# Re-timed seams of a four-stage transformer layer: tree weights, widened reciprocals, normalization steps and diagonal masks

## The chip, the cores and the metric

One core of one Trainium2 chip runs one program. The metric is the device time in microseconds (us), the median of three runs. TensorE (PE) multiplies matrices into the eight banks of PSUM; VectorE (DVE), ScalarE (ACT) and GpSimd (POOL) do the rest; SyncE (SP), ACT and POOL issue DMAs. Each engine works through its own list in order, and semaphores tie the lists together.

## The reference, cut to what matters

```python
# x: 2 x 1024 x 256, context: 2 x 77 x 256, all fp32, 16 heads of 16
x = x + block(layernorm(x))         # causal self-attention (diagonal included), a scan of
                                    # 8 steps xs, vs <- tanh(ctx @ w_ctx + xs @ w_x + b), and an MLP
x = x + cross_attention(layernorm(x), context)
x = x + trees(layernorm(x))         # 8 binary trees of depth 7: silu(logit) * (node on path) @ W_out
# inside block:
scores = where(causal, -inf, q @ k.T / 4); attn = softmax(scores) @ v
x = x + (attn @ out_w + out_b); x = x + scan(layernorm(x))
x = x + gelu(layernorm(x) @ ff_w1 + ff_b1) @ ff_w2 + ff_b2
```

## The kernel before, in words

The program is one list of instructions per engine, written out by hand, over a transposed residual stream `res` of 2 x 128 partitions by 2048 tokens in four chunks (c = 0 to 3) of 512. Products that must be exact are done as three products of a high and a low part (`three`, lines 347 to 351), so weights and activations are split: one engine rounds to the high part and another subtracts to get the low part.

**Self-attention.** It runs in eight rounds (`XQUADS`, n = 0 to 7), each for four heads of one batch element. A round has 12 steps; a step computes scores on PE (L1743, twice two matmuls), exponentiates on ACT (L867), zeroes the upper triangle of diagonal blocks on POOL (L699) and weighs the values on PE (L1760). Beside this, the row maxima for the next rounds are found: `unit(n, u)` multiplies one 128 x 128 block of queries and keys for four heads into one of the banks 5, 6, 7 (L1721), and `maximum(n, u)` on DVE reduces the 128 x 512 bank to four columns of `part_max` (L1171). A round has 36 units, eight of them on the diagonal: u = 0, 2, 5, 9, 14, 20, 27, 35. For these, `unit` adds a second matmul (L1724) that accumulates the causal mask through an identity. The units of round n + 1 from u = 8 and the first eight (`LEAD`) of round n + 2 are spread over the steps of round n; `gather` (L1180) and `negate` (L1187) finish a round's maxima on DVE, with `turn`, a transpose on PE, between them. A unit waits until the bank's previous user, three before it, has been read.

**MLP.** For each chunk c, PE does eight units m of the first matmul (`ff1`, six matmuls each), ACT applies Gelu (L996) and rounds (`hid_hi`, L999), DVE subtracts (`hid_lo`, L1411), and PE does eight units k of the second matmul (`ff2`). The layernorm of a later chunk is run beside it: `total`, `mean`, `center` (L1114), `square` (L780), `total_squares` (L1123), `variance` (L1647), `deviation` (L788, a square root, for which ACT loads another table than for Gelu), `invert` (L1131), `spread_out` (L1662), `scale` (L1140), and for ln3 `third_high` and `third_low` (the split of the normalized rows). The place of each of them among m and k sets the order. In chunk 0 three layernorms (ln3 of chunks 1, 2 and 3) are in flight, and POOL adds `x0` (L729) and builds `kbd` and `xk2` (L734, L740).

**Cross-attention.** It has 16 steps g (two for each n). A step has scores, an exponential, `cross_unit` with `cross_max` (L1888, L1386) for round n + 2, and `cross_weigh` (L1920). SP loads the queries of n + 2 (`load_q`, L585, six DMAs), the negated maxima (`load_neg`, L591) and packs the numerators of n - 1 (`pack_values`, L611, four DMAs). For batch element 0 the softmax denominators come back without HBM: `invert_cross` takes reciprocals (L1458), `widen` multiplies them with `own_part` into 128 x 1024 (L1464, 1.23 us on DVE), `denominators(j)` on PE (L1933) adds them up by head with `same_head` as weights, and `normalize_part(j)` multiplies (L1483). `denominators(2)` and `(3)` need `widen(1)`. `cross_project` (L1946) follows from g = 11.

**Trees.** The weights of eight trees come by `load_tree(t)` (L598, 512 KB each) into buffers that earlier stages have left, and `split_weights(t)` on POOL splits them (L721, L723). `spread_cross(2)` and `(3)` are POOL's DMAs for batch element 1 (L750, L752).

## Time and profile before

| what | value |
|---|---|
| median of 3 runs | 894.53 us (893.73 to 896.83) |
| the profiled execution | 893.74 us, its span 892.0 us |
| PE busy | 865.2 us (97%) |
| DVE, ACT, POOL busy | 575.7, 489.6, 176.2 us |
| mean granted clock of TensorE | 0.998 of full speed |

The span is what the profile shows; 1.7 us of the profiled execution lie outside it. Each engine's busy time counts overlapping instructions once. A matmul's row lasts longer than its place in the queue: the distance to the next row's start is its slot.

### The profile page before, as it was taken

The numbers are of one execution on the slowest core, as the hardware profiler recorded it, in microseconds if no ns is written. First come the engines' busy times: TensorE is split into PE (matmuls) and PEld (weight loads), VectorE is DVE, ScalarE is ACT, GpSimd is POOL, SyncE is SP. The second block draws the span as 40 slices with busy tenths as digits, with TensorE's granted clock in tenths as the row PEclk, the third lists the DMA queues.
The fourth block names the chain that finished last, engine by engine and source line by source line (L and its number), as shares of the span: only waits on it lengthen the run. The fifth ranks groups of instructions, "written<-read, shape, count | busy, mean of one in ns | idle before, by whom it ended". The sixth has DMA issues, their size and how long they took to land.

```text
span 892.0 us, 11261 instructions
## 1 busy us (share of the span) xinstructions
PE 865.2 (97%) x3967; PEld 526.4 (59%) x3967; DVE 575.7 (65%) x864; ACT 489.6 (55%) x715; POOL 176.2 (20%) x207
## 2 busy tenths in 40 slices
PE   9999999999999999999999999999899999999998
PEld 4665545545455545544446778774345777777775
DVE  4778757757777426678878774366654566665554
ACT  3536566566566755766657555437657433444332
POOL 8712332323222311000011630000015700000000
PEclk9999999999999999999999999999999999999999
DMA  4314405515524114200000000114656200000000
GB/s 148 67 37 75 85 13 98 96 25 96 108 51 93 31 34 165 96 0 1 0 0 22 1 1 1 35 37 87 137 112 156 67 1 25 1 24 1 1 24 24
DMA packets 21879, 46.28 MB, mean 52 GB/s; under 512 B 7896, under 2 KB 10840, under 8 KB 21440
## 3 DMA queue, kind: packets, MB, share of 16 engines
q1 hardware_dynamic: 19136, 43.17, 21.4%
q10 hardware_dynamic: 2080, 1.27, 0.6%
q0 software_dynamic: 608, 1.12, 0.6%
q8 instruction: 33, 0.54, 0.3%
q14 instruction: 22, 0.18, 0.1%
HBM read 17.04 MB, written 2.29 MB: 22 GB/s over the span
## 4 chain that ended last, share of the span: by engine, by line
PE 84%; DVE 5%; ACT 3%; issue 2%; DMA 2%; POOL 1%; SPq 1%; ACTq 0%; DVEq 0%; POOLq 0%
PE psum L1959 12%; PE psum L1721 9%; PE psum L349 9%; PE psum L350 8%; PE psum L351 8%; PE psum L1760 8%; PE psum L1743 8%; PE psum L1687 3%; PE psum L1662 2%; PE psum L1873 2%; PE psum L1724 2%; PE psum L1647 1%; PE psum L1639 1%; PE psum L1946 1%; PE psum L2162 1%
## 5 line engine op out<-in xcount | busy, mean ns | idle before, releaser
L1171 DVE TENSOR_REDUCE part_max<-psum 128x4 f32<-128x512 f32 x288 | 185.5, 686 | 71.0 <-PE psum L1721 56.4
L867 ACT ACTIVATE prob<-psum 128x1024 f32<-128x1024 f32 (+1 forms) x192 | 145.4, 809 | 85.9 <-PE psum L1743 85.4
L1721 PE MATMUL psum<-k,nat_hi 128*128 128x512 f32 x288 | 119.0, 452 | 2.5 <-ACT nat_lo L814 1.2
L1743 PE MATMUL psum<-q,k 128*128 128x512 f32 (+3 forms) x384 | 96.3, 354 | 0.3 <-ACT prob L867 0.3
L1079 ACT ACTIVATE silu<-psum,wt_bias 128x512 f32<-128x512 f32 x64 | 40.5, 684 | 101.9 <-PE psum L351 93.7
L1721 PEld LDWEIGHTS psum<-k,nat_hi 128*128 128x128 f32 x288 | 50.9, 188 | 62.7 <-issue 50.7
L699 POOL TENSOR_SCALAR_AFFINE_SELECT prob<-prob 128x256 f32<-128x256 f32 x128 | 52.3, 415 | 166.0 <-ACT prob L867 164.8
L1760 PE MATMUL psum<-prob,vq 128*32 128x512 f32 (+3 forms) x768 | 81.8, 498 | 1.3 <-POOL prob L699 1.2
L1743 PEld LDWEIGHTS psum<-q,k 128*128 128x128 f32 x384 | 65.2, 189 | 20.5 <-ACT prob L867 8.6
L1580 DVE TENSOR_TENSOR masked_lo<-masked,masked_hi 128x1024 fp32r<-128x1024 f32 x32 | 41.4, 1295 | 42.1 <-ACT masked_hi L1086 42.1
L349 PE MATMUL psum<-masked_hi,wt_hi 128*128 128x512 f32 x128 | 56.2, 439 | 1.2 <-DVE masked_lo L1580 1.2
L1959 PE MATMUL psum<-nrm,early 128*128 128x512 f32 x128 | 57.1, 593 | 0.0
L1959 PE MATMUL psum<-act_u,early 128*128 128x512 f32 x128 | 57.1, 593 | 0.0
L349 PE MATMUL psum<-tree_hi,wt_hi 128*128 128x512 f32 x128 | 53.6, 419 | 3.5 <-POOL wt_lo L723 2.9
L350 PE MATMUL psum<-nrm_lo,wt_hi 128*128 128x512 f32 x128 | 50.3, 393 | 0.0
L351 PE MATMUL psum<-masked_hi,wt_lo 128*128 128x512 f32 x128 | 50.1, 391 | 0.0
L350 PE MATMUL psum<-masked_lo,wt_hi 128*128 128x512 f32 x128 | 49.9, 390 | 0.0
L351 PE MATMUL psum<-tree_hi,wt_lo 128*128 128x512 f32 x128 | 49.9, 390 | 0.0
L1569 DVE TENSOR_SCALAR decide<-psum,wt_bias 128x512 bf16<-128x512 f32 x32 | 24.0, 750 | 39.7 <-PE psum L351 39.6
L1959 PEld LDWEIGHTS psum<-nrm,early 128*128 128x128 f32 x128 | 24.2, 190 | 29.7 <-issue 29.7
L1959 PEld LDWEIGHTS psum<-act_u,early 128*128 128x128 f32 x128 | 24.2, 190 | 29.7 <-issue 29.7
L1386 DVE TENSOR_REDUCE xrow_max<-psum 128x4 f32<-128x312 f32 x64 | 29.0, 477 | 18.4 <-PE psum L1888 17.9
(181 smaller groups left out, 1597.5 us busy)
## 6 DMA issues: line engine op xcount, KB each, us to landing
k<-nat_hi SPq DMA_DIRECT2D x92, 64.0 KB, 2.3
xq<-xq_b SPq DMA_DIRECT2D x36, 128.0 KB
q<-nat_hi SPq DMA_DIRECT2D x32, 128.0 KB, 2.3
wt<-in_wt SPq DMA_DIRECT2D x8, 512.0 KB, 4.0
nrm<-in_xT SPq DMA_DIRECT2D x4, 512.0 KB, 8.8
k<-nat_lo SPq DMA_DIRECT2D x32, 64.0 KB, 2.3
q<-nat_lo SPq DMA_DIRECT2D x16, 128.0 KB, 2.3
nrm<-stage SPq DMA_DIRECT2D x32, 64.0 KB, 2.3
```

Source lines behind the costliest of these rows:

```text
L349: pe.matmul(out, rounded(w_hi), rounded(x_hi), start=start, stop=False)
L350: pe.matmul(out, rounded(w_hi), rounded(x_lo), start=False, stop=False)
L351: return pe.matmul(out, rounded(w_lo), rounded(x_hi), start=False, stop=stop)
L699: pool.affine_select(out=blk, in_=blk, compare_op=ALU.is_ge, fill=0.0, base=0, pattern=[[0, 2], [1, P]], channel_multiplier=-1)\
L867: act.activation(prob[:, s % 2, p, :, q0:CH], psum[:, 2 * p:2 * p + 2, q0:CH], ACT.Exp, scale=SCALE)\
L1079: act.activation(silu[:, st.buf, half, :], bank(logit_bank(st.g, half)), ACT.Silu, bias=wt_bias[:, st.tree, half:half + 1]).then_inc(silu_ ...
L1171: dve.tensor_reduce(part_max[:].rearrange("q (j p i) k -> q p j i k", j=2, p=2)[:, :, :, i, kt], bank(5 + unit_slot[n, u] % 3).rearrange(" ...
L1580: dve.tensor_tensor(rounded(masked_lo[:, st.buf]), masked[:, st.buf], masked_hi[:, st.buf], ALU.subtract)\
L1721: mm = pe.matmul(heads, rounded(nat_hi[:, m, i * P:(i + 1) * P]), k1[:, qd, :, kt * P:(kt + 1) * P], start=True, stop=i != kt)
L1743: mm = pe.matmul(bank(2 * p + j)[:, q0:CH], k2[:, qd, p, j, kt * P:(kt + 1) * P], q2[:, qd, p, c * CH + q0:(c + 1) * CH], start=True, stop ...
L1760: mm = pe.matmul(psum[32 * h:32 * h + 32, 4, q0:CH], vq[:, qd, kt, h, :], prob[:, s % 2, h // 2, h % 2, q0:CH], start=first, stop=last)
L1959: mm = pe.matmul(bank(2 * c + m), wx01[:, k, m * P:(m + 1) * P], state(n)[:, k, cols_of(c)], start=False, stop=k == 1, skip_group_check=True)
```

## The change

1. Masks: except for round 0 and the first eight units of round 1, the mask matmul is left out. `maximum` of a diagonal unit becomes four `tensor_tensor_reduce` of 128 x 128, each of which adds `caus_f` to one head's block in PSUM, writes it back and puts its maximum in one column of `part_max`. That is 53 units (5 of round 1, 8 in each of rounds 2 to 7).
2. Start: 12 idle matmuls instead of 14.
3. MLP, chunk 0: Gelu of m = 0 to 2 goes ahead of ln3(1)'s square and root, which move in between them; the roundings of m = 0 to 2 come after Gelu 3; ln3(1)'s variance and spread move two units later, and for chunks 0 and 1 the variance and spread beside ff2 move from k = 1, 3 to k = 3, 5. ln3(3)'s `center` and `total_squares` move forward on DVE, its `square` goes ahead of ln3(2)'s `deviation` on ACT.
4. Cross-attention: `widen` moves to POOL, as `widen(0)`, `split_weights(0)`, `widen(1)`, `split_weights(1)`. `own_part` and `same_head` are made in the MLP. `invert_cross(1)` moves to the end of g = 9, and parts 0 and 1 of the denominators from g = 7, 8 to g = 8, 9.
5. Trees: loads 0, 1, 2, 3 are issued at n = 3, 4, 6, 6 instead of 5, 6, 7 and after; the buffers of trees 4, 5 and 6, 7 are exchanged, with their waits.

```diff
-        tree_w += late_w[1] + late_w[0] + late_w[2]
+        tree_w += late_w[1] + late_w[2] + late_w[0]
+        def masked_in_psum(n, u):
+            return self_units[u][0] == self_units[u][1] and (n == 0 or (n == 1 and u < LEAD))
...
-                if n == 5:
+                if n == 3:
                     sp.wait_ge(xq2_in[0], q_loaded(3))
                     load_tree(0)
+                if n == 4:
+                    load_tree(1)
                 if n == 6:
-                    load_tree(1)
-                if n == 7:
                     sp.wait_ge(xq2_in[1], q_loaded(7))
                     load_tree(2)
+                    load_tree(3)
             pack_values(XQUADS - 1)
-            load_tree(3)
-            sp.wait_ge(xpv_ps, 2 * XQUADS)
+            sp.wait_ge(xo_ps, 2 * KT)
             for t in (4, 5):
                 load_tree(t)
-            sp.wait_ge(xo_ps, 2 * KT)
+            sp.wait_ge(xpv_ps, 2 * XQUADS)
...
+            def widen(i):
+                pool.wait_ge(part_set, 1)
+                pool.wait_ge(xrec, i + 1)
+                pool.tensor_tensor(quot_b[0][:, 1, i, :]..., xrecip[:, i, :]..., own_part[:]...,
+                                   ALU.mult).then_inc(xspread, 1)
+            widen(0)
             split_weights(0)
+            widen(1)
+            split_weights(1)
             spread_cross(2)
-            split_weights(1)
...
-            square(ln3)(1)
-            deviation(ln3)(1)
+            def hidden_after(c, m):
+                return (() if m < 3 else (0, 1, 2) if m == 3 else (m - 1,)) if c == 0 else (m - 1,) if m > 0 else ()
...
+                    if c == 0 and m == 1:
+                        square(ln3)(1)
+                    if c == 0 and m == 2:
+                        deviation(ln3)(1)
+                    for i in hidden_after(c, m):
...
+                if c == 0:
+                    square(ln3)(3)
                 deviation(norm)(nc)
...
+                if i == kt and not masked_in_psum(n, u):
+                    for p in range(2):
+                        for j in range(2):
+                            at = (2 * p + j) * P
+                            ins = dve.tensor_tensor_reduce(
+                                psum[:, 5 + unit_slot[n, u] % 3, at:at + P],
+                                psum[:, 5 + unit_slot[n, u] % 3, at:at + P], caus_f[:], 1.0, -3e38,
+                                ALU.add, ALU.max, accum_out=part_max[:, 16 * j + 8 * p + i, kt:kt + 1])
+                    ins.then_inc(mx_free, 1)
+                    return
...
+                    if m == 5 and c == 2:
+                        head_tables()
...
+                if c == 0:
+                    center(ln3)(3)
                 invert(norm)(nc)
                 if c == 0:
-                    center(ln3)(3)
+                    total_squares(ln3)(3)
                 scale(norm)(nc)
...
-                if g in (6, 14):
-                    invert_cross({6: 0, 14: 2}[g])
-                if g == 6:
-                    widen(0)
-                if g in (7, 8, 10):
-                    normalize_part({7: 0, 8: 1, 10: 3}[g])
+                if g in (6, 9, 14):
+                    invert_cross({6: 0, 9: 1, 14: 2}[g])
+                if g in (8, 9, 10):
+                    normalize_part({8: 0, 9: 1, 10: 3}[g])
...
-            run_on(14)
+            run_on(12)
...
-                               start=True, stop=i != kt)
-                if i == kt:
+                               start=True, stop=not masked_in_psum(n, u))
+                if masked_in_psum(n, u):
...
-                    if c == 0 and m == 2:
+                    if c == 0 and m == 4:
                         variance(ln3)(1)
-                    if c == 0 and m == 4:
+                    if c == 0 and m == 6:
                         spread_out(ln3)(1)
-                    if m == (4, 4, 1, 1)[c]:
+                    if m == (5, 4, 1, 1)[c]:
...
-                    if k == (1, 1, 0, 0)[c]:
+                    if k == (3, 3, 0, 0)[c]:
                         variance(norm)(nc)
-                    if k == (3, 3, 2, 2)[c]:
+                    if k == (5, 5, 2, 2)[c]:
                         spread_out(norm)(nc)
-                    if c == 0 and k in (5, 7):
-                        (variance, spread_out)[(k - 5) // 2](ln3)(3)
+                    if c == 0 and k in (6, 7):
+                        (variance, spread_out)[k - 6](ln3)(3)
...
-                if g in (7, 8, 10):
-                    denominators({7: 0, 8: 1, 10: 3}[g])
+                if g in (8, 9, 10):
+                    denominators({8: 0, 9: 1, 10: 3}[g])
```

## Rows read from the trace of the kernel before

**Rows 1.** The page: busy time of each engine.
```profile
PE 865.2 (97%) x3967; PEld 526.4 (59%) x3967; DVE 575.7 (65%) x864; ACT 489.6 (55%) x715; POOL 176.2 (20%) x207
```
**Rows 2.** Windows: length, busy (x instructions) by engine, clock, DMA share, GB/s.
```profile
262.00:293.00 31.00, 30.75 (x191) 16.61 (x191) 24.20 (x39) 19.12 (x26) 7.74 (x18) 1.00 0.40 79
...
485.00:536.00 51.00, 46.76 (x219) 37.38 (x218) 38.28 (x51) 31.05 (x48) 22.57 (x14) 0.97 0.03 8
...
640.00:670.00 30.00, 27.51 (x128) 11.82 (x120) 17.72 (x32) 15.97 (x20) 4.52 (x3) 1.00 0.54 120
```
**Rows 3.** Who PE waited for, whole span: us in total, times, longest.
```profile
PE psum L1888 <- DVE xrow_max L1386: 3.7, 5, 1.6
...
PE psum L349 <- POOL wt_lo L723: 2.9, 2, 2.0
...
PE psum L1721 <- DVE part_max L1171: 0.6, 2, 0.4
```
**Rows 4.** Timeline of PE, a diagonal unit: start, length, instruction, in round 5.
```profile
253.85 0.40 PE L1721 MATMUL psum<-k,nat_hi 128*128 128x512 f32 x1
254.09 0.39 PE L1724 MATMUL psum<-causal_b,ident_b 128*128 128x512 bf16 x1
```
**Rows 5.** Groups of DVE, shapes apart: busy, mean ns, idle before.
```profile
L1171 DVE TENSOR_REDUCE part_max<-psum 128x4 f32<-128x512 f32 x288 | 185.5, 686 | 71.0 <-PE psum L1721 56.4 <-PE psum L1724 13.4
...
L1131 DVE RECIPROCAL rs<-sd 128x4 f32<-128x4 f32 x16 | 2.8, 174 | 6.5 <-ACT sd L788 6.5
...
L1187 DVE TENSOR_SCALAR neg_max<-psum 32x128 fp32r<-32x128 f32 x8 | 2.2, 270 | 0.4 <-PE psum L1733 0.4
...
L1304 DVE SCALAR_TENSOR_TENSOR early<-psum,vec,early 128x156 fp32r<-128x156 f32 x2 | 0.7, 374 | 0.0
```
**Rows 6.** Timeline of DVE in the same round.
```profile
252.65 2.56 DVE L1171 TENSOR_REDUCE part_max<-psum 128x4 f32<-128x512 f32 x4 [0.56 <-PE psum L1721]
...
261.55 0.42 DVE L1180 TENSOR_REDUCE row_max<-part_max 128x32 f32<-128x256 f32 x1
```
**Rows 7.** Timeline of PE: first scores of step 8 and of the next round.
```profile
259.00 0.63 PE L1743 MATMUL psum<-q,k 128*128 128x512 f32 x2
...
269.04 0.62 PE L1743 MATMUL psum<-q,k 128*128 128x512 f32 x2
```
**Rows 8.** Timeline of POOL at the start.
```profile
11.51 0.29 POOL L659 CAST ident_b<-ident 128x128 bf16<-128x128 f32 x1 [3.07 <-DMA caus_f<-in_causal]
```
**Rows 9.** Timeline of PE in the MLP, chunks 0 and 1.
```profile
486.83 0.50 PE L349 MATMUL psum<-nrm_hi,wff_hi 128*128 128x512 f32 x1 [0.85 <-ACT hid L996]
...
499.80 1.05 PE L1647 MATMUL psum<-mean_w,wide 128*128 128x1 f32 x8 [1.84 <-DVE wide L1123]
...
528.09 1.05 PE L1647 MATMUL psum<-mean_w,wide 128*128 128x1 f32 x8 [1.55 <-DVE wide L1123]
...
531.25 0.63 PE L349 MATMUL psum<-hid_hi,wff_hi 128*128 128x512 f32 x1
```
**Rows 10.** Timeline of DVE in chunk 0.
```profile
489.41 1.41 DVE L1140 SCALAR_TENSOR_TENSOR nrm<-nrm,vec,psum 128x512 f32<-128x512 f32 x2 [1.18 <-PE psum L1662]
```
**Rows 11.** Timeline of SP in cross-attention.
```profile
639.61 0.67 SPq L591 DMA_DIRECT2D xq<-neg_max  x1
...
655.08 0.58 SPq L598 DMA_DIRECT2D wt<-in_wt  x1
```
**Rows 12.** Timeline of POOL: the first split.
```profile
658.95 1.04 POOL L721 CAST wt_hi<-wt 128x1024 fp32r<-128x1024 f32 x1 [136.98 <-DMA wt<-in_wt]
660.07 2.70 POOL L723 TENSOR_TENSOR wt_lo<-wt,wt_hi 128x1024 fp32r<-128x1024 f32 x1
```
**Rows 13.** Timelines of DVE and PE about the second widening.
```profile
644.53 1.23 DVE L1464 TENSOR_TENSOR quot_b<-xrecip,own_part 128x1024 f32<-128x1024 f32 x1
```
```profile
646.30 0.38 PE L1888 MATMUL psum<-kbd,xq_b 128*128 128x312 f32 x1 [1.58 <-DVE xrow_max L1386]
...
647.38 1.08 PE L1933 MATMUL psum<-quot_b,caus_f 128*128 128x512 f32 x2
```

More of the change, by code:

```diff
@@ L754, in spread_cross @@
                     .then_inc(xden_in, 16)
+            def widen(i):
+                pool.wait_ge(part_set, 1)
+                pool.wait_ge(xrec, i + 1)
+                pool.tensor_tensor(quot_b[0][:, 1, i, :].rearrange("p (s n) -> p s n", s=HD),
+                                   xrecip[:, i, :].rearrange("p (o n) -> p o n", o=1).to_broadcast([P, HD, SEQ // HD]),
+                                   own_part[:].rearrange("p (s o) -> p s o", o=1).to_broadcast([P, HD, SEQ // HD]),
+                                   ALU.mult).then_inc(xspread, 1)
+            widen(0)
             split_weights(0)
+            widen(1)
+            split_weights(1)
             spread_cross(2)
-            split_weights(1)
             for t in (2, 3):
@@ L996, in _ @@
                         act.activation(hid[:, m, :], bank(ff1_bank(m)), ACT.Gelu, bias=v_("ffb1", m)).then_inc(gelu, 1)
-                    if m > 0:
-                        act.wait_ge(gelu, FT * c + m + 4)
-                        act.activation(rounded(hid_hi[:, m - 1, :]), hid[:, m - 1, :], ACT.Copy).then_inc(hid_h, 1)
+                    if c == 0 and m == 1:
[3 more added lines that the diff above has]
+                    for i in hidden_after(c, m):
+                        act.wait_ge(gelu, FT * c + i + 5)
+                        act.activation(rounded(hid_hi[:, i, :]), hid[:, i, :], ACT.Copy).then_inc(hid_h, 1)
                     if m == 6 and c == 0:
@@ L1014, in _ @@
                 if c == 0:
-                    square(ln3)(3)
                     third_high(2)
@@ L1373, in _ @@
             context_values()
+            add_state(2)
             total_squares(ln3)(1)
@@ L1397, in cross_neg, with head_tables @@
                     .then_inc(xmx_free, 1)
+            def head_tables():
+                dve.tensor_reduce(own_part[:], ident[:].rearrange("p (h s) -> p s h", s=HD), AX_X, ALU.add)\
+                    .then_inc(part_set, 1)
+                dve.wait_ge(consts, 2)
+                dve.tensor_copy(same_head[:].rearrange("p (h u) -> p h u", u=HD),
+                                vec[:, VEC["hmask"][0]:VEC["hmask"][0] + HT].rearrange("p (h u) -> p h u", u=1)
+                                .to_broadcast([P, HT, HD])).then_inc(part_set, 1)
             for c in range(NCH):
                 norm, nc = norm_beside(c)
-                if c == 0:
-                    add_state(2)
                 total(norm)(nc)
                 if c == 0:
+                    add_state(3)
                     invert(ln3)(1)
-                    add_state(3)
                     total(ln3)(3)
@@ L1424, in _ @@
                 if c == 0:
-                    center(ln3)(3)
+                    total_squares(ln3)(3)
                 scale(norm)(nc)
                 if c == 0:
-                    total_squares(ln3)(3)
                     third_low(2)
@@ L1458, in invert_cross @@
                 dve.reciprocal(xrecip[:, i, :], xsums[:, i, :]).then_inc(xrec, 1)
-            def widen(i):
-                dve.wait_ge(part_set, 1)
-                dve.wait_ge(xrec, i + 1)
-                dve.tensor_tensor(quot_b[0][:, 1, i, :].rearrange("p (s n) -> p s n", s=HD),
-                                  xrecip[:, i, :].rearrange("p (o n) -> p o n", o=1).to_broadcast([P, HD, SEQ // HD]),
-                                  own_part[:].rearrange("p (s o) -> p s o", o=1).to_broadcast([P, HD, SEQ // HD]),
-                                  ALU.mult).then_inc(xspread, 1)
-            def join_heads():
-                dve.wait_ge(consts, 2)
-                dve.tensor_copy(same_head[:].rearrange("p (h u) -> p h u", u=HD),
-                                vec[:, VEC["hmask"][0]:VEC["hmask"][0] + HT].rearrange("p (h u) -> p h u", u=1)
-                                .to_broadcast([P, HT, HD])).then_inc(part_set, 1)
             def normalize_part(j):
@@ L1507, in _ @@
                     xq_low(2, 0)
-                if g == 9:
-                    invert_cross(1)
-                    widen(1)
                 if g == 10:
@@ L1534, in _ @@
                     xq_low(3, g - 4)
-                if g in (6, 14):
-                    invert_cross({6: 0, 14: 2}[g])
-                if g == 5:
-                    dve.tensor_reduce(own_part[:], ident[:].rearrange("p (h s) -> p s h", s=HD), AX_X, ALU.add)\
-                        .then_inc(part_set, 1)
-                    join_heads()
-                if g == 6:
-                    widen(0)
-                if g in (7, 8, 10):
-                    normalize_part({7: 0, 8: 1, 10: 3}[g])
+                if g in (6, 9, 14):
+                    invert_cross({6: 0, 9: 1, 14: 2}[g])
+                if g in (8, 9, 10):
+                    normalize_part({8: 0, 9: 1, 10: 3}[g])
                 if g == 11:
```

## The prediction

> **What bounds the kernel now.** I read the page's busy times first: PE is busy 97% of the span, DVE 65% [rows 1]. So the time is PE's list plus the few places where it waits, and an edit helps only if it shortens that list or ends such a wait, and hurts if another engine can't follow. Cutting the span into windows shows the stages apart: in a self-attention round PE is busy 30.75 of 31 us and DVE 24.2; in the MLP's first chunks PE lacks 4.2 us of 51 and the clock is 0.97; in the middle of cross-attention it lacks 2.5 of 30 [rows 2]. The list of who PE waited for says for whom: 3.7 us for the maxima of cross-attention, 2.9 us for the trees' low parts, and only 0.6 us for the maxima of self-attention, where DVE is thus close behind but rarely late [rows 3]. The timelines then give the places and the slots.
>
> **Masks.** A mask matmul takes a slot of 0.24 us: the row after a unit's starts that much later, and both have 512 columns [rows 4]. 53 of them leave PE's list: 53 x 0.24 = 12.7 us is the most that this can give. In return DVE does four instructions of 128 x 128 where it did one reduce. The reduce is 0.686 us long but four of them in a row span 2.56, so its slot is (2.56 - 0.686) / 3 = 0.625 and 0.06 of each is hidden under the one before [rows 5, 6]. No row shows the new instruction. The nearest for its body is the 128-column TENSOR_SCALAR out of PSUM, 0.270 us, a slot of 0.21; a 156-column one with two inputs is 0.374 [rows 5]. Its maximum must also be brought out of the engine into `part_max`; if this is an instruction of its own, the nearest is the shortest one here, the reciprocal of four columns at 0.174, a slot of 0.11 [rows 5]. Low end: four bodies overlapped, 4 x 0.21 = 0.84 us for a unit. High end: neither hides anything, 4 x (0.270 + 0.174) = 1.78. I take 4 x (0.21 + 0.11) = 1.3, nearest to how short instructions stand here, so 0.67 more than the reduce.
>
> On this the Trainium skill speaks against the change: "VectorE: DVE Perf Modes" (Two Vector instructions with no wait between them) counts an instruction with an accumulator output as two, and its errata section gives 120 cycles plus the columns out of PSUM and 58 plus the columns otherwise, paid for each small tile. As an estimate from that page a unit costs 4 x (258 + 61) ns = 1.28 us; no row here shows the second instruction, and the sum above doesn't use it.
>
> A round without projections is about as long as the window of 31 us, in which DVE ran 39 instructions (36 units, `gather`, `negate` and one more) in 24.2 us [rows 2]. Eight diagonal units make DVE 24.2 + 8 x 0.67 = 29.6, while PE's list falls to 31 - 8 x 0.24 = 29.1. DVE becomes the bound of the round: not 1.9 but 1.4 us are won. The load is uneven too. Steps 8 to 11, from 259.00 to 269.04 [rows 7], hold 10 units, four of them diagonal, with `gather` (0.42) and `negate` (0.27) [rows 5, 6]: PE 10.04 - 0.96 = 9.1 us, DVE 10 x 0.625 + 0.69 + 4 x 0.67 = 9.6, and in step 8 alone two diagonals and `gather` stand ahead of the transpose that PE executes in order. With three banks PE is, by my estimate, 0.6 us late there each time. That leaves 0.8 us a round for rounds 0, 2, 4 and 5; rounds 1 and 3 have projections in steps 4 to 7 as cover, but the same end (1.9 - 0.5 - 0.6), 0.8 too. Round 6 has five diagonals, no early units and a free DVE: 5 x 0.24 = 1.2. Masks: about -6 us. With the low end -12.7. With the high end DVE needs 24.2 + 8 x 1.15 = 33.4 us a round, 2.4 more than now: four times that, 1.3 in each of two (steps 8 to 11: 11.5 of DVE against 10.04), less 1.2, is +11. The gain turns into a loss at 24.2 + 8 x = 31, x = 0.85, a unit of 1.47 us.
>
> **Start.** Two idle matmuls go, some 0.4 us each, but POOL's casts, and with them the first variance, wait for the mask's DMA until 11.51 [rows 8]. What is late next is that transfer: -0.15 us, bounds 0 and -0.8.
>
> **MLP.** In chunk 0 ff1 stood 0.85 us for Gelu 0 at 486.83 [rows 9], behind square, root and two table loads. Now Gelu 0 comes first, at 481, and that wait is gone. But the root of ln3(1) comes after m = 4, its spread after m = 6 (at about 491.9, where it was 488.5), and `scale(ln3)(1)` stands before all `hid_lo` on DVE. It began at 489.41 [rows 10]; at 491.9 it pushes the first `hid_lo` to 493.9, 0.6 us after PE gets there. The variance of ln3(2), which waited 1.84 us [rows 9], comes two units later, but the DVE list ahead of its `total_squares` (`hid_lo` beside POOL's adds of `x0`, and `third_low` behind a later `third_high`) is later by 3 us too: again some 1.9 us. And ACT now has `square(ln3)(3)`, which needs `center(3)` behind the last `hid_lo`, ahead of the root of ln3(2): its spread waits some 1.8 us. Against 0.85 + 1.84 now, 0.6 + 1.9 + 1.8: +1.2 us with the shorter distances at the end of the chunk counted. Chunk 1 is cleaner: its variance waits 1.55 us, and then eight matmuls run at twice their slot (0.43 for 0.23; one of their rows shows 0.63 for the 0.39 to 0.40 of rows 4's kind [rows 4, 9]), a cost of 1.6 us. Two units later there are 2.8 us more for DVE, so both go: -3.2. Sum -2.0; bounds -6 (chunk 0's waits gone too) and +1 (slow clock in chunk 0 after its longer waits). `head_tables` in chunk 2 costs DVE 0.5 us where it waits for ACT: nothing.
>
> **Cross-attention.** Taking `widen` (1.23 us [rows 13]) and the tables off DVE ends waits of PE for the maxima queued behind them: of the 3.7 us in five waits [rows 3] I put 3.1 down to them, 1.58 of it at 646.30, right behind the second `widen` [rows 13]. What takes their place is the order on POOL. SP goes from one issue to the next without a gap up to 639.61, when round 4 begins in its list [rows 11], so tree 0's load, the last of round 3, is issued just there. Its landing took 658.95 - 655.08 = 3.9 us [rows 11, 12]: it is there at 643.5. `split_weights(0)` takes 1.04 + 2.70 us [rows 12], to 647.3, and only then comes `widen(1)`, though its reciprocal is ready before 644.53, when DVE now starts the same product [rows 13]. On POOL a two-input subtraction of 128 x 1024 takes 2.4 to 2.7 [rows 12], so `widen(1)` ends at 649.8. `denominators(2)`, which now runs at 647.38 [rows 13] and would be reached at 644.3, stands at the head of PE's list: it waits 5.5 us and ends 2.5 later than now. Behind it stand scores, weighing and the projections of g = 11. After an idle stretch like that I expect the clock to fall as in chunk 1, another 1.6. Sum +4.1; bounds -3.1 (the load early, or the wait covered) and +5.
>
> **Trees.** Trees 2 and 3 are split before they are needed: of the two waits of 2.9 us in all [rows 3] the first, 0.9, goes. The second, 2.0, is for tree 4, whose split stands behind `spread_cross(3)` as before, and that waits for a reciprocal late in g = 0: it stays. -0.9; bounds 0 and -2.9. Three more DMAs ahead of SP's later loads cost issue time of 0.6 us each [rows 11]; the queries behind them are loaded a round ahead.
>
> **Sum.** -6 - 0.15 - 2.0 + 4.1 - 0.9 = -5.0 us, from 893.74 (span 892.0 and 1.7 around it) to 888.7; that execution lies 0.8 below the median of the runs, so 889 for the median.
>
> **Rivals.**
> - *No stall at the denominators.* If the load lands 4 us sooner, or PE is late itself, the 3.1 us are won instead: 889 - 7 = 882. For it: all else in the list is moved earlier. Against: SP's rows have no gap up to 639.61 [rows 11].
> - *Masks even out.* At 1.45 to 1.5 us a unit, DVE gives back all that PE wins: 889 + 6 = 895, within the measurement. For it: 24.2 of 31 us are DVE's already [rows 2].
> - *DVE becomes the bound, and slower than before.* At 1.78 us a unit +11 instead of -6: 906; it decides from 1.47 us up. For it: each of the 8 small instructions may pay its full length. Against: the reduces do overlap [rows 6].
> - *The small waits are only moved.* The MLP edits win nothing: 891.
>
> **How the numbers follow.** The forecast's case gets 0.40, no stall 0.20, masks even 0.16, DVE the bound 0.14, MLP nothing 0.10. A measurement here tells 0.3% (2.7 us) from no change. Faster by more: the first two, most of the last, 0.65. Within: 0.17. Slower: 0.18. The range reaches from the low case with cheap masks, 880, to the even case's upper side, 897; beyond it lie the dear masks and both good ends together, 0.2.
>
> **What would show it.** Rows of `part_max` of 128 x 128 at L1171's place: 4 x 53, with or without a partner that reads out; their four-block distance is the unit's price. Waits of L1721 or of the transpose for DVE, growing from 0.6 us to some 10 in all, mostly in step 8. L1933 waiting 5 us for POOL near the third denominator, with rows of double length behind it. No wait at 528 for a variance, but ones for variance and spread in chunk 0. One wt_lo wait of 2 us left. The prediction is wrong if the four-block price is off by more than 0.2 us, or if `widen(1)` isn't behind a split when PE comes.

## The result, and the profile after

893.62 us (median of 20, 890.50 to 895.94) against 895.44 (median of 20, 892.16 to 898.98) for the kernel before: a ratio of 0.9975, 95% interval 0.9963 to 0.9987. That is 2.2 us less, a quarter of a per cent, where 5.0 were forecast. The profiled execution has a span of 890.6 us where the kernel before had 892.0.

The two traces hold the same matmuls at most places, so the start of one in the trace after, less its start in the trace before, says where time went. All experiments below are read in the same way, always against the trace before.

| the matmul that starts | before | after | difference | part | its own | forecast |
|---|---|---|---|---|---|---|
| first weighing of self-attention | 71.61 | 71.23 | -0.38 | start | -0.4 | -0.15 |
| last weighing of self-attention | 322.55 | 317.48 | -5.07 | masks | -4.7 | -6 |
| MLP, chunk 0 | 479.18 | 474.12 | -5.06 | | | |
| MLP, chunk 1 | 511.64 | 509.52 | -2.12 | chunk 0 | +2.9 | +1.2 |
| MLP, chunk 2 | 539.79 | 534.24 | -5.55 | chunk 1 | -3.4 | -3.2 |
| cross-attention | 600.25 | 594.71 | -5.54 | | | |
| `denominators(2)` | 647.38 | 644.23 | -3.15 | | | |
| first output projection | 652.57 | 651.11 | -1.46 | cross | +4.1 | +4.1 |
| first tree | 676.72 | 676.19 | -0.53 | to the trees | +0.9 | |
| last matmul | 888.42 | 887.03 | -1.39 | trees | -0.9 | -0.9, with the row above |

The page of the kernel after, busy times, beside [rows 1]:
```profile
PE 857.5 (96%) x3896; PEld 522.1 (59%) x3912; DVE 589.4 (66%) x1233; ACT 490.7 (55%) x716; POOL 178.9 (20%) x209
```
PE's list is 7.7 us shorter than in [rows 1], though the clock was low for longer (it is a little too short: 55 instructions were taken out and 71 are missing), and the span only 1.4: the rest went into waits. Who PE waited for, whole span of the kernel after, beside [rows 3]:
```profile
PE psum L1951 <- POOL quot_b L764: 3.9, 1, 3.9
PE psum L1739 <- DVE part_max L1197: 2.2, 6, 0.5
PE psum L353 <- DVE masked_lo L1598: 1.9, 3, 0.8
PE psum L1751 <- DVE row_max L1212: 1.8, 7, 0.8
PE psum L1665 <- DVE wide L1145: 1.7, 1, 1.7
...
PE psum L353 <- POOL wt_lo L727: 1.2, 1, 1.2
PE psum L1926 <- DMA xq<-neg_max: 1.2, 1, 1.2
```
The waits for the maxima of cross-attention went from 3.7 to 0.8 us. In their place stand POOL's widening (3.9) and a transfer of maxima (1.2); the waits for the four-block units and for `gather` in self-attention (L1739, and the transpose L1751) are new, 4.0 in all; and the waits for `masked_lo` in the trees, 1.2 us before, are 1.9.

**The masks.** The two halves of the new unit among DVE's groups of the kernel after, and one unit in DVE's timeline:
```profile
L1197 DVE CUSTOM_DVE_ANT_0 psum<-psum,caus_f 128x128 f32<-128x128 f32 x212 | 55.0, 320 | 4.9 <-PE psum L1739 3.6
...
L1197 DVE DVE_READ_ACCUMULATOR2_ANT part_max<- 128x1 f32 x212 | 29.6, 139 | 0.0
```
```profile
257.27 0.42 DVE L1212 TENSOR_REDUCE row_max<-part_max 128x32 f32<-128x256 f32 x1
257.84 0.30 DVE L1197 CUSTOM_DVE_ANT_0 psum<-psum,caus_f 128x128 f32<-128x128 f32 x1
258.05 0.14 DVE L1197 DVE_READ_ACCUMULATOR2_ANT part_max<- 128x1 f32 x1
258.05 0.33 DVE L1197 CUSTOM_DVE_ANT_0 psum<-psum,caus_f 128x128 f32<-128x128 f32 x1
...
258.80 0.68 DVE L1203 TENSOR_REDUCE part_max<-psum 128x4 f32<-128x512 f32 x1
```
Each of the four instructions has a partner that reads the accumulator out, but the next body starts together with it: 0.25 us a block, 258.80 - 257.84 = 0.96 for the unit. (By "VectorE: DVE Perf Modes" of the Trainium skill, section "Two Vector instructions with no wait between them", such an instruction counts as two; the trace agrees, 212 of each. The prediction's estimate of 1.28 us a unit from that page's figures is too high here.) A reduce takes a slot of 0.625 [rows 5, 6], so eight units add 8 x 0.34 = 2.7 us to the 24.2 of [rows 2]. The window over the same round of the kernel after has 26.87:
```profile
257.40:287.60 30.20, 29.02 (x180) 15.45 (x179) 26.87 (x96) 18.99 (x26) 7.76 (x18) 1.00 0.41 82
```
**MLP, chunk 0.** The timeline of PE; the third row is the first of twelve between the variance and the spread:
```profile
488.97 0.47 PE L353 MATMUL psum<-hid_hi,wff_hi 128*128 128x512 f32 x1 [0.82 <-DVE hid_lo L1451]
...
497.21 1.55 PE L1665 MATMUL psum<-mean_w,wide 128*128 128x1 f32 x8 [1.68 <-DVE wide L1145]
...
499.19 0.63 PE L354 MATMUL psum<-hid_lo,wff_hi 128*128 128x512 f32 x1
...
503.89 1.31 PE L1680 MATMUL psum<-ident,rs 128*128 128x128 f32 x8
```
The waits are of 2.5 us in all, where [rows 9] had 0.85 and 1.84 in this chunk. What is new is behind them: rows of 0.63 us at a distance of 0.43, where they were 0.39 at 0.23. The same twelve took 503.56 - 500.72 = 2.84 us before and 503.89 - 498.62 = 5.27 now, 2.4 more. This is TensorE at 1.2 GHz and not 2.4; the window shows a granted clock of 0.50, with PE busy throughout:
```profile
497.60:504.40 6.80, 6.80 (x21) 5.64 (x22) 2.91 (x6) 2.60 (x3) 4.76 (x5) 0.50 0.01 1
```
Half of 6.8 is an estimate of 3.4 us for the whole stretch, the matmuls of the variance and the spread included, in a chunk that is 2.9 us longer although its waits are 0.2 shorter.

**Cross-attention.** POOL, then PE, about `denominators(2)`, beside [rows 12, 13]:
```profile
638.86 1.04 POOL L725 CAST wt_hi<-wt 128x1024 fp32r<-128x1024 f32 x1 [8.21 <-DMA wt<-in_wt]
639.98 2.34 POOL L727 TENSOR_TENSOR wt_lo<-wt,wt_hi 128x1024 fp32r<-128x1024 f32 x1
642.28 1.90 POOL L764 TENSOR_TENSOR quot_b<-xrecip,own_part 128x1024 f32<-128x1024 f32 x1
```
```profile
639.43 0.68 PE L1926 MATMUL psum<-xq,xk 98*77 98x512 f32 x2 [1.21 <-DMA xq<-neg_max]
...
640.10 0.27 PE L1915 MATMUL psum<-ident,xrow_max 128*32 128x128 f32 x1
644.23 2.08 PE L1951 MATMUL psum<-quot_b,caus_f 128*128 128x512 f32 x2 [3.86 <-POOL quot_b L764]
645.32 1.84 PE L1926 MATMUL psum<-xq,xk 98*77 98x512 f32 x2
```
The widening stands behind the split, PE stands at the denominators, and the matmuls behind are of double length (2.08 for the 1.08 of [rows 13]).

### The profile page after: what moved, and what is told of

Same layout as the page of the kernel before. It is cut to its first block, busy times and chain, and to the rows that moved or that the text cites. A ratio compares the mean times of both kernels' runs of the same rounds, so it can differ in the third digit from the quotient of the medians.

```text
span 890.6 us, 11506 instructions
## 1 busy us (share of the span) xinstructions
PE 857.5 (96%) x3896; PEld 522.1 (59%) x3912; DVE 589.4 (66%) x1233; ACT 490.7 (55%) x716; POOL 178.9 (20%) x209
## 4 chain that ended last, share of the span: by engine, by line
PE 78%; DVE 6%; SPq 4%; ACT 3%; issue 3%; DMA 3%; POOL 1%; ACTq 0%; DVEq 0%; POOLq 0%
PE psum L1977 12%; PE psum L353 9%; PE psum L354 9%; PE psum L355 9%; PE psum L1739 7%; PE psum L1778 6%; PE psum L1761 6%; PE psum L1705 3%; PE psum L1680 2%; PE psum L1657 2%; DVE part_max L1203 2%; PE psum L1665 2%; SPq L507 1%; PE psum L1964 1%; PE psum L1891 1%
## 5 line engine op out<-in xcount | busy, mean ns | idle before, releaser
L1203 DVE TENSOR_REDUCE part_max<-psum 128x4 f32<-128x512 f32 x235 | 151.8, 686 | 44.6 <-PE psum L1739 41.1
L1739 PE MATMUL psum<-k,nat_hi 128*128 128x512 f32 x288 | 116.2, 444 | 5.2 <-DVE part_max L1197 2.2
L1739 PEld LDWEIGHTS psum<-k,nat_hi 128*128 128x128 f32 x288 | 49.8, 188 | 68.5 <-issue 57.0
L1197 DVE CUSTOM_DVE_ANT_0 psum<-psum,caus_f 128x128 f32<-128x128 f32 x212 | 55.0, 320 | 4.9 <-PE psum L1739 3.6
L1977 PEld LDWEIGHTS psum<-act_u,early 128*128 128x128 f32 x128 | 24.2, 190 | 29.7 <-issue 29.7
```

The lines of the kernel that those rows point to most:

```text
L1197: ins = dve.tensor_tensor_reduce(psum[:, 5 + unit_slot[n, u] % 3, at:at + P], psum[:, 5 + unit_slot[n, u] % 3, at:at + P], caus_f[:], 1.0, ...
L1203: dve.tensor_reduce(part_max[:].rearrange("q (j p i) k -> q p j i k", j=2, p=2)[:, :, :, i, kt], bank(5 + unit_slot[n, u] % 3).rearrange(" ...
L1739: mm = pe.matmul(heads, rounded(nat_hi[:, m, i * P:(i + 1) * P]), k1[:, qd, :, kt * P:(kt + 1) * P], start=True, stop=not masked_in_psum(n ...
L1977: mm = pe.matmul(bank(2 * c + m), wx01[:, k, m * P:(m + 1) * P], state(n)[:, k, cols_of(c)], start=False, stop=k == 1, skip_group_check=True)
```

## The experiments

Single executions unless a ratio is given. One time by itself says little, since the change's own 20 go from 890.5 to 895.9 us; the readings rest on rows and on differences of the table's kind.

**widen_first.** Does the order on POOL cause the loss?
```diff
             widen(0)
-            split_weights(0)
             widen(1)
+            split_weights(0)
             split_weights(1)
```


> The changed kernel with one line moved: on GpSimd the second widening stands ahead of the first split instead of behind it. Theory (the order on GpSimd makes PE wait 3.9 us at the third denominator and slows its clock behind it): that wait is gone, L1951 follows the transpose at once, no matmul of double length behind it, and the span is 4 to 5.5 us shorter than the changed kernel's 890.6. Rival (the numerators' DMA or the reciprocal would be late at that place anyway): PE waits there for DVE or a DMA instead, and the span is less than 2 us shorter.

887.66 us. The wait of 3.9 is 0.8, no matmul behind it is slow, and from the start of cross-attention to the first projection it takes 0.7 us more than before, not 4.1. But the 3.1 us of waits that ended are not won: PE now waits for two transfers there, the maxima and the packed values ahead of DVE's `normalize_part`. (Chunk 0, which this edit doesn't touch, is 1.5 us shorter than in the change: see the account at the end.) Its timeline:
```profile
638.10 0.69 PE L1926 MATMUL psum<-xq,xk 98*77 98x512 f32 x2 [1.37 <-DMA xq<-neg_max]
...
639.81 1.12 PE L1951 MATMUL psum<-quot_b,caus_f 128*128 128x512 f32 x2 [0.77 <-POOL quot_b L764]
...
643.88 1.10 PE L1951 MATMUL psum<-quot_b,caus_f 128*128 128x512 f32 x2 [1.00 <-DVE quot_b L1510]
```
**widen_first_timed.** The same kernel in rounds.

> The change with widen(1) ahead of the first split, timed in rounds. By its trace it ends 4.8 us ahead of the change (1.5 of that stands in the first chunk of the feed-forward part, where the clock came back sooner, and isn't due to the edit). By the theory, which has the stall behind the split cost 2.5 us and a slow clock of 1.6 to 4, the time is 2.5 to 4.5 us under the change's 893.6, a ratio to before of 0.992 to 0.995. By the rival (the single look was a lucky execution, and what the wait took is spent in waits for transfers) it is under 1 us, 0.9965 or more.

888.19 us (887.25 to 893.96), ratio 0.993 (0.9903 to 0.9956): the edit is worth some 4 us against the ratio 0.9975. The executions show the clock at work: one at a mean granted clock of 0.998 took 887.63, one at 0.990 took 892.77. The change itself has the same spread: the eight of its 20 executions at 0.996 have a median of 891.6, the seven at 0.992 one of 893.7.

**two_in_psum.** Step 8 is late because two diagonal units and `gather` stand in a row on DVE. Two of the eight go back to TensorE, the last of a round and the first of the next.
```diff
-            return ... and (n == 0 or (n == 1 and u < LEAD))
+            return ... and (n == 0 or (n == 1 and u < LEAD) or u in (0, SUNITS - 1))
```


> The changed kernel, but the last and the first diagonal unit of every round (u = 35 and u = 0), which stand on both sides of the row maxima's gather and the transpose, keep their mask matmul. Theory (the masks' gain is lost in step 8 alone, where two masked units and the gather stand in a row on DVE ahead of the transpose): step 8, now 0.40 us longer than before the change and 0.58 in round 6, comes back to its old length or less; 6 x 0.4 + 0.6 = 3 us shorter in all, with no change in the other steps. Rival (DVE is the bound of the whole round): the time saved on DVE, 0.4 us a unit and 0.8 a round, shows in all steps. Second rival (PE pays for the two matmuls in full and nothing comes back): 13 x 0.24 = 3 us longer.

891.35 us; the self-attention is 7.46 us shorter than before in place of 4.69. The distance from weighing k to the next, less that of the kernel before (us, mean of rounds 0 to 5; then round 6 alone). Between weighings 7 and 8 stand the last two units of step 8 and the transpose of the gathered maxima, and then the scores of step 9:

| k | 0 | 3 | 4 | 6 | 7 | 8 | 10 | round |
|---|---|---|---|---|---|---|---|---|
| the change | -0.22 | -0.06 | -0.23 | -0.23 | **+0.42** | -0.23 | -0.21 | -0.75 |
| two_in_psum | -0.22 | -0.06 | -0.23 | 0 | **-0.23** | -0.22 | -0.22 | -1.15 |
| the change, round 6 | -0.21 | -0.10 | -0.22 | -0.23 | **+0.58** | 0 | 0 | -0.19 |
| two_in_psum, round 6 | -0.21 | -0.10 | -0.23 | 0 | **0** | 0 | 0 | -0.54 |

Two masks cost TensorE 0.24 each again and end what was lost in step 8: 6 x 0.40 + 0.35 = 2.8 us. `gather` and the transpose behind it, in the kernel after and in this one (DVE and PE of each):
```profile
257.75 0.28 PE L1751 MATMUL psum<-ident,row_max 128*32 128x128 f32 x1 [0.17 <-DVE row_max L1212]
...
259.08 0.47 PE L1739 MATMUL psum<-k,nat_hi 128*128 128x512 f32 x1 [0.34 <-DVE part_max L1197]
```
```profile
255.32 0.42 DVE L1212 TENSOR_REDUCE row_max<-part_max 128x32 f32<-128x256 f32 x1
```
```profile
256.29 0.27 PE L1751 MATMUL psum<-ident,row_max 128*32 128x128 f32 x1
```
With two units masked by TensorE `gather` is done 0.5 us ahead of the transpose, which waits for nothing.

**chunk0_begin.** The first chunk of the MLP begins as before (order of Gelus, roundings, ln3(1), and on DVE `add_state(2)` and `invert(ln3)(1)`, two moves of the change that its list above doesn't name); all else is the change. The diff is cut; where a line moves, mostly its new place is shown.
```diff
+            square(ln3)(1)
+            deviation(ln3)(1)
...
-                return (() if m < 3 else (0, 1, 2) if m == 3 else (m - 1,)) if c == 0 else (m - 1,) if m > 0 else ()
+                return (m - 1,) if m > 0 else ()
...
+                if c == 0:
+                    add_state(2)
...
+                    invert(ln3)(1)
                     add_state(3)
...
-                    if c == 0 and m == 4:
+                    if c == 0 and m == 2:
                         variance(ln3)(1)
-                    if c == 0 and m == 6:
+                    if c == 0 and m == 4:
                         spread_out(ln3)(1)
-                    if m == (5, 4, 1, 1)[c]:
+                    if m == (4, 4, 1, 1)[c]:
...
```


> The changed kernel, but the first half of chunk 0 of the MLP is as before the change (square, root, variance and spread of ln3's chunk 1 early; roundings one behind Gelu); its second half and chunk 1 stay changed. Theory (the later spread of ln3(1) holds back all of DVE's list by 2 to 3 us, so that the variance of ln3(2) waits in spite of its later place, and the slow clock follows): no wait at that variance, no slow clock in chunk 0; 0.85 us for Gelu comes back; chunk 0 takes 30 to 31 us instead of 35.0 and the span is 4 to 5 us shorter. Rival (the wait at the variance is due to the second half's own order): it stays at some 1.7 us, and the span changes by less than 1.

891.66 us. Chunk 0 is 1.0 us shorter than before in place of 2.9 longer. The waits of PE there:
```profile
482.46 0.50 PE L353 MATMUL psum<-nrm_hi,wff_hi 128*128 128x512 f32 x1 [0.85 <-ACT hid L1015]
500.75 1.16 PE L1679 MATMUL psum<-ident,rs 128*128 128x128 f32 x8 [0.81 <-DVE rs L1151]
```
and no slow clock (granted 1.00 from 480 to 505 us, where the kernel after had 0.86). The wait of 1.84 for the variance is gone, and only now shows the later one, for the spread, that was forecast. The joined kernels and early_half below have the same beginning: chunk 0 is 1.0 us shorter in all three, with no slow clock. It is a group of moves that was put back, and which of them counts was not tried.

**split_waits.** Do POOL's early splits of trees 2 and 3 slow DVE's low part of tree 0?
```diff
+            pool.wait_ge(ln5.scaled, 2)
             for t in (2, 3):
                 split_weights(t)
```


> The changed kernel, but GpSimd starts the splits of trees 2 and 3 only when the first low part of the trees' rows (tree_low(0)) is done. Theory (GpSimd's early splits hold up that DVE subtraction, 2.50 us for two instead of 1.55, and PE waits 1.0 us for it at the first logits): that wait goes, the pair takes 1.4 to 1.6 us, the span is about 1 us shorter, if both splits still end in time (3.5 us each, needed 8 and 11 us later). Rival (the wait at the first logits is ACT's exponential, as the profile names it): 1.0 us stays.

894.00 us. From the first projection to the first tree: +0.2 in place of +0.9. The same instruction in the kernel after and in this one (DVE):
```profile
673.59 2.50 DVE L1524 TENSOR_TENSOR nrm_lo<-nrm,tree_hi 128x512 fp32r<-128x512 f32 x2 [1.06 <-ACT tree_hi L1070]
```
```profile
676.32 1.29 DVE L1525 TENSOR_TENSOR nrm_lo<-nrm,tree_hi 128x512 fp32r<-128x512 f32 x2 [1.05 <-ACT tree_hi L1071]
```
Without POOL beside it, half as long. ("SBUF — State Buffer" of the Trainium skill, section on the two separate sides, has VectorE with two inputs in SBUF and GpSimd exclude each other there; the rows agree.) The time was no better, since the slow clock behind `denominators(2)` lasted longer in this execution: cross-attention +6.6 in place of +4.1.

**masks_alone.** The kernel before with the masks' part of the change alone.

> The kernel before, and of the whole change only the masks: the 53 diagonal units outside round 0 and the early units are reduced by four VectorE instructions each, and everything else stands as it stood. The theory from the profile after: a round wins 0.83 us and the sixth 0.2, in all 4.7, though each step 8 is 0.6 to 0.8 us late, and nothing behind the self-attention moves. It expects the self-attention 4.7 us shorter, the same matmul starts as before less 4.7 at every later anchor to within 0.5, a time of 4 to 5 us less than before, a ratio of 0.9945 to 0.996. First rival: the masks' gain is eaten later by whatever bounds the start of the feed-forward part (a transfer or a queue that doesn't come sooner): under 2 us at the end. Second rival: the other edits of the change (two idle matmuls less, the start) had a part in the 4.7: a self-attention that is less than 4 us shorter.

890.26 us, ratio 0.9943 (0.9921 to 0.9966). The self-attention is 4.61 us shorter, and the difference then stays between 4.4 and 5.1 to the end. By its trace the masks give 5.1 us where the whole change gives 1.4: everything else in it costs 3.7 together. By the ratios it is 5.1 against 2.2, so 2.9, and the two intervals just touch.

**neg_first.** With widen(1) first, the maxima's transfer (16 KB) was issued 0.6 us behind a tree's load (512 KB), and PE had it 4.6 after its issue. Here the loads of trees 0 and 1 stand right behind it.
```diff
                     load_neg(n + 1)
+                if n == 4:
+                    sp.wait_ge(xq2_in[0], q_loaded(3))
+                    load_tree(0)
+                if n == 5:
+                    load_tree(1)
...
-                if n == 3:
-                    sp.wait_ge(xq2_in[0], q_loaded(3))
-                    load_tree(0)
-                if n == 4:
-                    load_tree(1)
```


> The change with widen(1) ahead of the first split, and the loads of trees 0 and 1 right behind the next round's maxima in SP's queue. For the trace: by the theory TensorE's 1.4 us for the maxima's transfer goes, and from the start of the cross-attention to its first projection it takes 0.7 + 1.4 less than with the loads ahead: 0.7 us less than before the change instead of 0.7 more. By the rival (SP's queue itself is the bound there) the packed values land no sooner, TensorE's waits for VectorE's product grow from 1.0 to 2 us or more, and the distance stays at +0.3 to +0.7.

893.74 us. The wait for the maxima is gone and both others grew, in PE's timeline:
```profile
640.69 1.12 PE L1951 MATMUL psum<-quot_b,caus_f 128*128 128x512 f32 x2 [2.22 <-POOL quot_b L764]
648.55 2.04 PE L1951 MATMUL psum<-quot_b,caus_f 128*128 128x512 f32 x2 [4.79 <-DVE quot_b L1510]
```
Cross-attention takes 5.7 us more than before, where 0.7 less was expected. The packed values behind that product were issued from 639.33 and used at 647.72, 8.4 us later (4.7 with the loads ahead); tree 1's load was issued 0.8 us behind the last of them. The rival was right in kind and far too small in size.

**loads_as_before.** widen(1) first, and all loads of the trees, with their buffers and waits, as in the kernel before, so that none stands in rounds 3 and 4 of SP's list.
```diff
-                if n == 3:
+                if n == 5:
                     sp.wait_ge(xq2_in[0], q_loaded(3))
                     load_tree(0)
-                if n == 4:
-                    load_tree(1)
...
```


> The change with widen(1) ahead of the first split, and the loads of the trees back at the places that they had before (tree 0 in round 5 of SP's list, two rounds later). The theory: with no 512 KB transfer ahead of them, the maxima and the packed values of rounds 4 and 5 land sooner, so both waits of the kernel with widen(1) first (1.4 us for the maxima, 1.0 for VectorE's product behind the packed values) shrink to under 0.5 each, and from the start of the cross-attention to the first projection it takes 1 us less than before in place of 0.7 more. The rival: what holds this stage is SP's list with 14 issues a round, or the distance of the denominators themselves, and the waits stay: +0.3 to +0.7. In time 1 to 2 us less than the kernel with widen(1) first by the theory, the same by the rival; the trees may take back 0.9, since their splits come later.

893.58 us, ratio 0.9975 (0.9956 to 0.9994). Both waits for transfers are gone, and the one for POOL is 2.2. PE, then the window behind it, then PE at the trees:
```profile
639.74 2.07 PE L1951 MATMUL psum<-quot_b,caus_f 128*128 128x512 f32 x2 [2.22 <-POOL quot_b L764]
```
```profile
640.00:650.00 10.00, 9.95 (x23) 3.96 (x24) 3.22 (x6) 2.64 (x3) 0.00 (x0) 0.52 0.66 130
```
```profile
684.96 0.79 PE L353 MATMUL psum<-tree_hi,wt_hi 128*128 128x512 f32 x1 [3.83 <-POOL wt_lo L727]
```
`denominators(2)` starts 7.64 us ahead of before, with the loads two rounds earlier it was 7.57. The widening on POOL began at 637.78, when its reciprocal was there, takes 1.90 us and holds PE at the same place; the waits for transfers only stood ahead of it. Then the clock was 0.52 of full for 10 us, so that from the start of cross-attention to the first projection it takes 3.0 us more than before, where 1 less was expected; and the late splits cost a wait of 3.8 more.

**joined** and **joined_neg.** widen_first, two_in_psum, chunk0_begin and split_waits in one; the second with neg_first's edit too.

> The change with all four repairs together: widen(1) ahead of the first split, two of the units of each round masked by TensorE again, the splits of trees 2 and 3 behind the low part of tree 0, and the first chunk of the feed-forward part as before. If each keeps what its single look showed it to win (4.7 by widen_first at the end of the trace, 2.8 of the self-attention by two_in_psum, 3.9 of the first chunk by chunk0_begin, 0.7 between projection and trees by split_waits), it ends 12 us ahead of the change: about 881 to 882 us, a ratio of 0.985 against before. The rival is that TensorE, when it comes to the cross-attention sooner and waits for nothing there, is held by the queue of SP, whose rounds were without a gap already, so that part of the cross-attention's gain is not to be had twice: 884 to 886.

> As the joined kernel, and the loads of trees 0 and 1 (512 KB each) stand in SP's queue right behind the next round's maxima (16 KB) in place of right ahead of them. The theory: with widen(1) first, TensorE waits 1.4 us for the transfer of the maxima, which was issued 0.6 us behind a tree's load and landed 4.6 us after its issue, because it shares the DMA engines with the load. It expects that wait gone and 1 to 1.4 us less than the joined kernel. The rival: SP issues 14 transfers a round one after the other for 7.5 to 8 us, which is about what a round lasts, so the wait only moves to the packed values (VectorE's product behind them, 1.0 us now) and the time stays within 0.5 us of the joined kernel.

joined: 883.24 us, ratio 0.986 (0.9842 to 0.9878), between the two expectations. joined_neg: 882.42, ratio 0.9853 (0.9834 to 0.9871). Both reach cross-attention 12.1 us ahead of before, and end 9.2 and 10.6 ahead. A part of what that stage takes back is the clock. The same ten us in joined, and in joined_neg, whose list on PE is the same:
```profile
600.00:610.00 10.00, 9.60 (x43) 5.49 (x39) 3.28 (x8) 7.09 (x9) 0.00 (x0) 0.60 0.53 109
```
```profile
600.00:610.00 10.00, 9.38 (x58) 5.01 (x55) 5.35 (x13) 8.69 (x11) 0.00 (x0) 1.00 0.53 109
```
That cost joined 3.8 us; ahead of it PE waits in both for DVE alone, 0.26 us at 599.0. The two kernels can't be told apart in time, so the 1 to 1.4 us that were expected of the second didn't show; in joined_neg the maxima's wait (0.9) is gone, and those for POOL (1.3 to 2.2) and DVE (0.5 to 1.8) grew.

**early_half.** The repaired self-attention and MLP, with cross-attention and trees of the kernel before.

> Only what the change does up to the end of the feed-forward part, with two of its repairs (two units of a round masked by TensorE, the first chunk's first half as before); cross-attention, the trees' loads and their splits stand as in the kernel before. The theory: the joined kernels reach the cross-attention 12.1 us ahead of before and lose 2.3 to 3.7 of it up to the first tree, since widening on GpSimd and loads two rounds earlier are no gain even with widen(1) first; with the old arrangement the distance stays at 12 us and the end comes 11.5 to 12.5 ahead, a ratio of 0.985 to 0.9865 and 1 to 2 us less than the joined kernels' 882 to 883. The rival: the old cross-attention loses too when it is reached 12 us sooner (its transfers bound it), and ends no more than 10 us ahead, 884 or more.

882.68 us, ratio 0.9845 (0.9821 to 0.987). It is 12.2 us ahead at the start of cross-attention and 11.0 at the end; PE waits 2.5 us there for DVE's maxima, in three waits, and the clock is low from 621.7 to 628.5. In time it can't be told from the joined kernels, where 1 to 2 us less were expected. So the change's cross-attention, even with its order repaired, is worth nothing that was measured.

## Why the prediction was wrong

The forecast was 5.0 us less; the trace has 1.4 less and the medians 1.8, or 2.2 by the ratio. The direction and the place of the largest stall were right, and three terms of the sum were mis-sized, all on the hopeful side. The sign of error that the prediction named came true: the four-block price is off by 0.34 us.

- **MLP, chunk 0: +1.2 forecast, +2.9 measured.** The waits themselves came out lower than written: 2.5 us against 0.6 + 1.9 + 1.8, and 2.7 before. The step that failed is that no slow clock was counted behind them; it stood only in the upper bound. It cost 2.4 us on twelve matmuls (shown by the rows) and 3.4 by estimate in all, and with the old beginning it is gone (shown by chunk0_begin). How much it costs differs from one execution to the next. Seven traces have this beginning, with the same two waits (0.8 and 1.65 to 1.71 us), and the clock fell behind the second in all of them: for 6.8 us in the change and split_waits, which makes the chunk 2.9 longer, and for 3.4 us in the other five, where it is 1.5 to 1.9 longer. That those five come near the forecast's +1.2 is luck: it counted 1.6 us more of waits and no slow clock, and they have shorter waits and a slow clock. The third wait of the forecast, for ln3(2)'s spread, did not appear; the likely reason is that the slow matmuls covered it, since chunk0_begin, which has none, waits 0.81 there, and two of the five with the shorter slow clock wait 0.2.
- **Masks: -6 forecast, -4.7 measured.** The step that failed is round 6: "five diagonals, no early units and a free DVE: 5 x 0.24 = 1.2". It gave 0.2, because diagonals and `gather` stand in a row in step 8 of that round too (+0.58 there, with one mask fewer). In rounds 0 to 5 the sum was near, 0.75 for 0.8, by two errors that cancel. The unit costs DVE 0.96 us and not 1.3, so DVE is no bound of the round (26.87 of 30.20 us); and step 8 is late by 0.9 (0.42 + 2 x 0.24) and not 0.6. A mean over a round did not say it, a list of what stands in a row in one step did; two_in_psum shows it. PE's waits for this work came to 4 us more and not to some 10.
- **Trees: -0.9 forecast, +0.1 measured.** Two steps failed. The first is that the end of a wait was counted as a gain in full, with nothing behind it. The wait of 0.9 for POOL went, but a little later, at 688.32, PE now waits 0.7 for DVE's `masked_lo`. That the trees are 0.9 shorter all the same is due to the second wait for POOL, 1.25 us in place of 2.0, and this isn't the change's doing: masks_alone, with the trees of the kernel before, waits 1.03 and 1.28 there and is 0.66 shorter from the first tree to the end. Of the edit itself some 0.2 is left. The second step is that POOL's work moves next to DVE's: DVE's low part of tree 0 took 2.50 us beside POOL's early splits, where it took 1.55 in the kernel before, and 0.9 is lost ahead of the trees. split_waits gets 0.7 of it back, and loads_as_before, where the splits come later, has 1.29 for the same rows and loses 0.3.
- **Cross-attention: +4.1 forecast, +4.1 measured**, with the place, the releaser and the slow matmuls as written. The parts differ: POOL's product took 1.90 us and not 2.4 to 2.7, the wait was 3.9 and not 5.5, but 1.2 of wait for the maxima's transfer, not foreseen, stood ahead of it. That the sum fits is partly luck: the errors cancel, and in the three other kernels with this order on POOL (two_in_psum, chunk0_begin, split_waits) the same stretch took 6.1, 6.4 and 6.6 us more than before, with the clock low for 10.2, 13.7 and 13.7 us where the change had 6.8. widen_first shows the order as the cause: 4.1 becomes 0.7, and 0.5 in the trace of widen_first_timed.
- **Chunk 1: -3.2 forecast, -3.4 measured:** right, with -3.4 in all eleven traces that have the later variance and 0.0 in masks_alone, which doesn't.
- **Start: -0.15 forecast, -0.4 measured:** not shown. Eleven traces with 12 idle matmuls begin weighing between 0.5 us sooner and 0.4 later than the kernel before, and masks_alone, which has 14, 0.1 sooner.

Of the rivals, "no stall at the denominators" and "DVE becomes the bound" did not happen. The time lies between "the small waits are only moved" (891) and "masks even out" (895), but the first holds in part only (the MLP won 0.5, and masks and trees fell short besides), and the second not at all (a unit costs 0.96).

What stays open: why neg_first's packed values took 8.4 us (the loads beside them are the likely cause: tree 0's, issued at 635.07, landed at 641.80, and tree 1's at 650.62; they weren't taken away alone), and why one execution goes to the low clock near 600 us, behind 0.26 us of wait, and another with the same list and the same wait doesn't.

## What to carry to other kernels

Where PE is 97% busy, price each new wait with the slow matmuls that may stand behind it as well as its length, and as a range: behind a wait of 1.7 us the low clock cost an estimated 1.7 to 3.4 here (half of 3.4 to 6.8 us), behind one of 3.9 some 1.8 (from 644.2 to 647.8) and more in other executions, and behind the 1.84 of [rows 9] nothing. When work moves from TensorE to VectorE, don't judge it by a round's mean; find the step where several of the dearer pieces and a reduction stand in a row ahead of something that PE executes in order, and leave what you can of that step where it was. And a change of many edits should be run in parts: here one part alone gave more than the whole, by its trace and by its median.

## What the runs showed of the hardware

- The same kernel differs by 5 us between executions (887.63 and 892.77) with the mean granted clock (0.998 and 0.990): whether and how long matmuls run at half speed behind a wait is not fixed. Behind one and the same wait of 1.65 to 1.71 us the clock was low for 3.4 us in five traces and for 6.8 in two. Cross-attention with the stall lost 4.1, 6.1, 6.4 and 6.6 us in four kernels that have it.
- Two instructions with an accumulator out of PSUM, 128 x 128, follow each other at 0.25 us, although each is 0.32 long and has a partner of 0.14.
- While POOL split a tree's weights (a cast to the high part and subtractions of 128 x 1024), two DVE subtractions of 128 x 512 with both inputs in SBUF took 2.50 us together, against 1.29 without it. POOL's cast took 1.49 there for 1.04 elsewhere, and its next subtraction 2.71 for 2.34 to 2.38.
